# Copying the transposed causal attention weights of both octets on ScalarE, none on VectorE

## What is computed

```python
scores = jnp.einsum('bhid,bhjd->bhij', q, k)
rel = jnp.einsum('bhid,pd->bhip', q, rel_key)
rel_idx = jnp.clip(j - i + p - 1, 0, p - 1)
bias = jnp.take_along_axis(rel, ..., axis=3)
logits = jnp.where(causal[None, None], (scores + bias) * scale, -jnp.inf)
attn = jax.nn.softmax(logits, axis=-1)
out = jnp.einsum('bhij,bhjd->bhid', attn, v)
...
x = x + _layernorm(_L0_attn_ref(_layernorm(x), ...))   # causal attention
x = x + _layernorm(_L0_ffn_ref(_layernorm(x), ...))    # gated feed-forward, silu
x = x + _layernorm(_L1_attn_ref(_layernorm(x), ...))   # quaternion attention
x = x + _layernorm(_L1_ffn_ref(_layernorm(x), ...))    # 8 experts, 2 per token
```

## Time and profile before

| | us |
|---|---|
| median of 3 runs | 986.7 |
| lowest and highest | 984.15, 988.79 |
| the profiled execution | 992.06 |
| its span in the profile | 990.0 |

### The profile page before, as it was taken

The page is one execution under the profiler, slowest core; times in us unless marked ns, Lnnn a source line. Parts: engine busy times, 40 slices in busy tenths (PEclk is TensorE's granted clock), DMA queues, the critical chain, the costliest instruction groups (busy, mean ns, idle before and its releaser), DMA issues.

```text
span 990.0 us, 21425 instructions
## 1 busy us (share of the span) xinstructions
PE 776.4 (78%) x8384; PEld 558.3 (56%) x8384; DVE 499.9 (50%) x1656; ACT 456.7 (46%) x885; POOL 177.1 (18%) x306
## 2 busy tenths in 40 slices
PE   1678887787887889998998976788787767488994
PEld 0466766565765566665665654366443545267773
DVE  3266556556645465545446562647454536423315
ACT  1234352235454547665556653556844445332321
POOL 3200101000010000020000004233005553115411
PEclk9999999699997999998899997999977989979998
DMA  4400200000400001300000212011131110011101
GB/s 109 156 2 2 121 2 2 2 1 2 151 2 5 8 13 32 99 23 2 12 12 1 87 43 74 20 31 32 42 121 49 46 49 27 6 30 38 38 20 35
DMA packets 36440, 38.29 MB, mean 39 GB/s; under 512 B 8982, under 2 KB 26220, under 8 KB 36212
## 3 DMA queue, kind: packets, MB, share of 16 engines
q1 hardware_dynamic: 34548, 33.65, 11.3%
q0 software_dynamic: 1536, 3.15, 1.1%
q10 hardware_dynamic: 256, 0.13, 0.0%
HBM read 19.87 MB, written 16.91 MB: 37 GB/s over the span
## 4 chain that ended last, share of the span: by engine, by line
PE 51%; DVE 21%; issue 13%; ACT 8%; another core or an unknown queue 2%; ACTq 1%; DMA 1%; POOL 1%; SPq 0%; POOLq 0%; DVEq 0%
PE ps L1542 5%; PE ps L1687 5%; PE ps L1557 4%; PE ps L1545 4%; PE ps L1702 4%; PE ps L1470 3%; PE ps L1570 3%; PE ps L1762 3%; PE ps L1774 3%; ACT late L905 3%; DVE probsT L981 3%; PE ps L1637 2%; PE ps L1539 2%; DVE neg_max L1168 2%
## 5 line engine op out<-in xcount | busy, mean ns | idle before, releaser
L905 ACT ACTIVATE late<-ps,j_bias 128x512 f32<-128x512 f32 x256 | 173.3, 690 | 173.9 <-PE ps L1687 167.1
L1168 DVE TENSOR_REDUCE neg_max<-ps 128x2 f32<-128x32 f32 (+31 forms) x128 | 90.5, 707 | 147.8 <-PE ps L1548 143.4
L1687 PE MATMUL ps<-q_heads,k_parts 128*128 128x512 f32 x256 | 135.1, 546 | 22.1 <-ACT late L905 19.2
L832 ACT ACTIVATE probs<-ps,neg_max 128x16 f32<-128x16 f32 (+31 forms) x256 | 109.1, 483 | 23.7 <-DVE neg_max L1168 23.4
L756 ACT ACTIVATE probsT<-ps 128x128 f32<-128x128 f32 (+3 forms) x128 | 55.9, 437 | 126.8 <-PE ps L1557 113.1
L981 DVE COPY probsT<-ps 128x128 f32<-128x128 f32 (+3 forms) x173 | 75.1, 434 | 60.6 <-PE ps L1557 25.6
L1542 PE MATMUL ps<-kT_two,q_wide 64*64 64x262 f32 (+16 forms) x1024 | 74.3, 355 | 36.7 <-DVE probsT L981 26.2
L629 POOL TENSOR_TENSOR q_wide<-qT,eighth_mask 128x1024 f32<-128x1024 f32 x16 | 31.2, 1951 | 395.1 <-PE ps L1548 220.3
L1557 PE MATMUL ps<-ident,probs 128*128 128x128 f32 x640 | 96.9, 283 | 1.0 <-ACT probs L832 1.0
L1687 PEld LDWEIGHTS ps<-q_heads,k_parts 128*128 128x128 f32 x256 | 50.5, 205 | 71.9 <-ACT late L905 50.6
L1557 PEld LDWEIGHTS ps<-ident,probs 128*128 128x128 f32 x640 | 76.1, 144 | 16.6 <-issue 9.4
(11 more groups left out here) (265 smaller groups left out, 1315.7 us busy)
## 6 DMA issues: line engine op xcount, KB each, us to landing
k_parts<-k_half SPq DMA_DIRECT2D x16, 256.0 KB, 3.1
q_parts<-q_half SPq DMA_DIRECT2D x16, 256.0 KB, 3.5
k_parts<-k_parts SPq DMA_DIRECT2D x16, 256.0 KB, 3.1
q_heads<-q_parts SPq DMA_DIRECT2D x64, 64.0 KB, 2.1
x_by_expert<-q_heads SPq DMA_DIRECT2D x3, 960.0 KB, 7.6
probsT<-x_by_expert SPq DMA_DIRECT2D x45, 64.0 KB, 1.8
y_by_expert<-probsT SPq DMA_DIRECT2D x45, 64.0 KB
late<-in_L_ffn_w_dram SPq DMA_DIRECT2D x1, 2048.0 KB
```

What stands on the lines that cost most here:

```text
L832: nc.scalar.activation(probs[:, k, 0:L], ps[:, k, 0:L], ACT.Exp, bias=neg_max[:, n % 4, o:o + 1]).then_inc(exp_ready.sem, 1)
L905: nc.scalar.activation(head_probs[:, i % SLOTS, :], ps[:, banks[i % len(banks)], :], ACT.Exp, bias=j_bias[:]).then_inc(e2_ready.sem, 1)
L1168: nc.vector.tensor_reduce(neg_max[:, n % 4, :], ps[:, k:k + OCT, 0:QS * (n + 1)], axis=AXX, op=ALU.max, negate=True).then_inc(max_ready.se ...
L1687: mm(ps[:, banks[i % R], :], k_parts[:, hg, kc * P:(kc + 1) * P], q_heads[:, hg % 2, g, :], start=True, stop=True).then_inc(s2_ready.sem, 1)
```

## The change

ScalarE's generator issues two copies for each step, octet 0's and then octet 1's, ahead of the exponentials of the next step. VectorE's generator issues none; its piece in the odd slot keeps only the work that some steps have there (`copy_outT`, `divide_tile`). The two semaphores are renamed from the engine to the octet, and both are now raised by ScalarE; the waits for them stand where they stood.

```diff
--- before.py
+++ after.py
@@ -374,8 +374,8 @@
         max_ready = Signal(sem("max_ready"), NST)
         exp_ready = Signal(sem("exp_ready"), OCT * NST)
         pT_ps = Signal(sem("pT_ps"), OCT * NST)
-        pT_dve = Signal(sem("pT_dve"), NST)
-        pT_act = Signal(sem("pT_act"), NST)
+        pT_first = Signal(sem("pT_first"), NST)
+        pT_second = Signal(sem("pT_second"), NST)
         av_ps = Signal(sem("av_ps"), T)
         outT_ready = Signal(sem("outT_ready"), T)
         turned_ps = Signal(sem("turned_ps"), T)
@@ -836,7 +836,8 @@
                 yield
                 for n in range(NST):
                     yield
-                    copy_pT(act, copy, 1, pT_act, b, n)
+                    copy_pT(act, copy, 0, pT_first, b, n)
+                    copy_pT(act, copy, 1, pT_second, b, n)
                     if n + 1 < NST:
                         exps(n + 1)
                     if n >= SPT and n % SPT == 2:
@@ -1174,7 +1175,6 @@
                     if n + 1 < NST:
                         maxima(n + 1)
                     yield
-                    copy_pT(dve, copy, 0, pT_dve, b, n)
                     if n >= SPT and n % SPT == 0:
                         copy_outT(b, n // SPT - 1)
                     if n >= SPT and n % SPT == 1:
@@ -1526,8 +1526,8 @@
                     pe.wait_ge(qwide_ready.sem, qwide_ready.at(b, t + 1))
                     pe.wait_ge(b7_free, fill_no["R", b, 4 * t + 2] + 1)
                 if b * NST + n >= 2:
-                    pe.wait_ge(pT_dve.sem, pT_dve.at(b, n - 1))
-                    pe.wait_ge(pT_act.sem, pT_act.at(b, n - 1))
+                    pe.wait_ge(pT_first.sem, pT_first.at(b, n - 1))
+                    pe.wait_ge(pT_second.sem, pT_second.at(b, n - 1))
                 L = QS * (n + 1)
                 kT, kT_far = kT_two[:, b % 2, :], kT_far_two[:, b % 2, :]
                 blocks = [2 * (n % SPT) + z for z in range(2)]
@@ -1559,8 +1559,8 @@
                     last.then_inc(pT_ps.sem, 1)
 
             def weigh_values(b, t):
-                pe.wait_ge(pT_dve.sem, pT_dve.at(b, (t + 1) * SPT))
-                pe.wait_ge(pT_act.sem, pT_act.at(b, (t + 1) * SPT))
+                pe.wait_ge(pT_first.sem, pT_first.at(b, (t + 1) * SPT))
+                pe.wait_ge(pT_second.sem, pT_second.at(b, (t + 1) * SPT))
                 if b * T + t:
                     pe.wait_ge(attnT_ready.sem, attnT_ready.at(b, t))
                 for k in range(HG):
@@ -1674,8 +1674,8 @@
                 if b >= 1:
                     pe.wait_ge(e2_ready.sem, e2_ready.at(b, 0))
                 if R > 1:
-                    pe.wait_ge(pT_dve.sem, pT_dve.at(B, 0))
-                    pe.wait_ge(pT_act.sem, pT_act.at(B, 0))
+                    pe.wait_ge(pT_first.sem, pT_first.at(B, 0))
+                    pe.wait_ge(pT_second.sem, pT_second.at(B, 0))
                 for i in range(NCH + 5):
                     hg, kc, g = i // (KC * GH), i // GH % KC, i % GH
                     if i < NCH:
```

## The result

The changed kernel takes 950.4 us (median of four executions, 948.6 to 956.0), the kernel before 985.4 (982.8 to 988.8): a ratio of 0.965, 95% interval 0.960 to 0.971. Two repeats gave 951.5 against 984.0 (0.965, 0.962 to 0.969) and 964.3 against 993.8 (0.970, 0.966 to 0.974). Times are medians of all executions; ratios are of the means, without the few executions that fell in a slower state of the chip. So the sign and the main mechanism were right, and the size was too small by 10 to 15 us.

What follows compares the result with a forecast made beforehand. No engine is full: TensorE's work and the waits between its pieces bound the kernel. Terms 11 + 5 + 5 + 3 + 0 - 4 = 20 us take the median 986.7 to 966.7 us; range 953 to 982.

Steps and rivals of the forecast that it cites:

- What bounds it, what moves: Causal rounds: 128 copies leave VectorE (56 us less) for ScalarE (56 more); scores' waits on ScalarE grow to 30 to 40.
- (a): Four turns of tokens behind a normalisation: scores are done earlier, so TensorE turns right after it; 11 us gained.
- (b): Feed-forward's second normalisation, three times: scores stop waiting and L1094, which frees bank 7, starts earlier; 5 us gained.
- (c): Head's normalisation, three times: scores no longer wait for VectorE's copy behind L1045 and a maxima; 5 us gained.
- (d): Gate pieces, six times, where L1200 stands before VectorE's copy: both copies done 0.5 us earlier; 3 us gained.
- (e): The other 28 or so waits of TensorE for VectorE: up to 8 us more gain, counted at nothing.
- (f): Cost where ScalarE has no idle time, and through its later exponentials in rounds 2 and 3: 4 us, ends 2 and 22.
- The spacing: On ScalarE, the instruction following a 512-column copy starts 0.50 us after the copy's start, not 0.60.
- Behind 594 us the work is the same and simply starts earlier: After the four causal rounds: unchanged work, with no gain of its own in the sum.
- The clock: Rival in the causal rounds: joined gaps keep the granted clock low longer, costing 10 us of the gain, 977; chance 0.04.
- The range: Whole kernel: 953 us, from a gain of 34 with small costs, to 982, where the wait is handed on.

Runs made afterwards that it cites:

- second and third pairs: Kernel before and changed kernel, each run and traced again without any edit: 951.5 against 984.0 us, then 964.3 against 993.8 us.

## Why the prediction was too small

- *What bounds it, what moves.* Right. No causal copy of `probsT` by VectorE is left (its first one, at 596.4 us, is the later stage's); the waits for ScalarE's copies are 30.0 us, at the lower edge of the 30 to 40 expected; rounds 1 and 3 are shorter by 9 to 12, rounds 0 and 2 by 1 to 5. "ScalarE 56 us more" was wrong: 39, since copies in a row overlap. "VectorE 56 us less" was 50, of copies that had taken 62.3.
- *(a)* 11 forecast, 8.0 to 10.4 measured, some 5 of it at equal clock in the second and third pairs. The turns, rounds 1 and 3 of the first trace of the changed kernel:

```profile
174.09 1.12 DVE L1046 TENSOR_SCALAR xn<-x_all,moments,rstd 128x128 f32<-128x128 f32 x4
174.59 1.16 PE L1423 MATMUL ps<-ident,xn 128*128 128x128 f32 x4 [4.61 <-DVE xn L1046]
...
554.84 1.11 DVE L1046 TENSOR_SCALAR xn<-x_all,moments,rstd 128x128 f32<-128x128 f32 x4
555.34 1.00 PE L1423 MATMUL ps<-ident,xn 128*128 128x128 f32 x4 [0.70 <-DVE xn L1046]
```

  The turn now ends 0.54 and 0.39 us after the normalisation (2.57 and 3.5 before), as argued. In round 1 the wait ahead of it is as long as ever, 4.61 us for 4.59: it changed its name, and the gain is the scores that no longer stand behind it. The shortfall is round 2, steps 7 to 10, which gained between -1.0 and 0.7 us for 2.5, with 7 to 10 us of low clock around this very turn in both kernels, and the last turn, which gained 2.5 us in two pairs (3.9 in the first) for 3.8.
- *(b)* The term that was mis-sized, as shown above: 5 forecast, 11.5 measured. 4.8 us are three stretches of low clock that went away with the gaps; the other 6.7 are two waits of the scores in each round, where the forecast had priced one.
- *(c), (d)* Right, within 1 us each.
- *(e), (f)* Together -4 forecast, -1.7 twice and 1.7 once. This is a small net of larger parts: the steps that became longer add up to 11 to 12 us in each pair, some of it from low-clock stretches that moved. A single case of 0.15 us per step in 18 steps was too little for (f), and nothing too little for (e): steps 24 of round 1 and 25 of round 3, in none of (a) to (d), gained 1.9 and 1.2 us. The two errors mostly cancelled. The spacing on which (f) rested holds. Two copies of 512 columns, which would be 1.20 us one after the other:

```profile
259.96 1.08 ACT L756 ACTIVATE probsT<-ps 128x512 f32<-128x512 f32 x2 [0.67 <-PE ps L1557]
```

  That is 0.48 us to the start of the second and 0.60 for the second, as long as one alone. The Trainium skill (VectorE: DVE Perf Modes, the section on the TRN2 errata) has a fixed part in every copy out of PSUM, which made an estimate of 0.57 us for the first; the trace shows it is not paid in full between two copies in a row.
- *"Behind 594 us the work is the same and simply starts earlier."* The rounds explain 24.7 of 32.5 us on one chip and 24.5 of 29.5 on the other, and 27.1 of 35.0 in the first result. The 5 to 8 us that remain are what the sum lacks besides the clock in the rounds, and their cause stays open. Part of them goes with the clock: within the executions of before on the three chips (23, 13 and 29) the time rises by 0.17, 0.34 and 0.25 us for each us of low clock, and the changed kernel has 34 and 20 us less of it on the first and the last chip (98 for 132, 125 for 145). 10 us of that vanish in the rounds, where they are already counted, so it would explain 24 x 0.17 = 4 and 10 x 0.25 = 2.5 us, if the slopes hold between kernels. The traces don't show it: outside the rounds the three pairs differ by 9.0, 0.2 and -0.5 us, and from the copy of the section below to the end it took 386.3, 376.8 and 378.7 us before and 378.9, 377.8 and 386.0 after, the same in the mean, with no less low clock.
- *The clock.* I had put it at a small chance of costing 10 us. In the rounds there was 10 us less of it, worth some 5 us. The sign of that rival was wrong. That less idleness may end the low stretches sooner stands beside it in the prediction, but the sum had no term for it.
- *The range.* Its lower end, 986.7 - 34, isn't the sum of its own parts: (a) to (d) with (e) in full and (f) at 2 give 24 + 8 - 2 = 30 us, 957. The miss of 3 us would have been 6.

## What to carry to other kernels

A copy that frees PSUM for the next matmuls costs what stands before it in its engine's queue, not its own 0.4 us: look for every place where it follows a chain of small dependent instructions, count all of them, and give it to the engine that would otherwise wait for the same matmuls. Here that engine was good for one more copy, hardly for two. And where TensorE's gaps vanish while the granted clock is low in places, put the low clock into the range as a gain too: here 10 us of it went, worth some 5.

## What was not expected of the hardware

While POOL issues its eight indirect DMAs, some 1.27 us apart, the other engines can stand still although what they wait for is done. The third trace of before, then the second of the changed kernel:

```profile
596.56 1.17 POOL L676 DMA_INDIRECT x_by_expert<-xn,row_no  x1 [64.28 <-DVE row_no L1313]
...
600.75 0.27 PE L1570 MATMUL ps<-probsT,v_two 128*9 128x128 f32 x1 [0.31 <-issue]
...
605.63 0.96 POOL L676 DMA_INDIRECT x_by_expert<-xn,row_no  x1 [0.30 <-issue]
607.97 0.62 SPq L536 DMA_DIRECT2D kT_far_two<-in_L_ffn_b_dram  x2
607.98 0.69 DVE L981 COPY outT<-ps 128x512 f32<-128x512 f32 x1 [11.71 <-remote]
608.00 0.95 POOL L684 MEMSET b_two<- 128x1024 f32 x1 [1.42 <-remote]
608.01 1.26 ACT L905 ACTIVATE late<-ps,j_bias 128x512 f32<-128x512 f32 x2 [14.48 <-remote]
```

```profile
572.28 1.17 POOL L676 DMA_INDIRECT x_by_expert<-xn,row_no  x1 [59.80 <-DVE row_no L1313]
573.42 0.63 SPq L536 DMA_DIRECT2D kT_far_two<-in_L_ffn_b_dram  x2
573.43 0.69 DVE L982 COPY outT<-ps 128x512 f32<-128x512 f32 x1 [1.45 <-PE ps L1570]
```

In the first, L1570's last matmul ends at 601.0, and the copy that waits for it starts at 607.98, in the same 0.05 us as the next instruction of ScalarE, POOL and SP. In the second it starts at once. From the first indirect DMA to this copy it took 1.2 or 2.8 us in the four traces on the chip where before took 984 us, and 4.3 to 11.5 us in the eight on the other two chips, with different kernels in either group. In the mean that is 5.6 us more, about half of what those chips take longer. In the first trace of before it was 4.3 us. The change doesn't touch this place, but it took 4.3, 2.8 and 11.4 us before and 2.8, 1.2 and 4.3 in the changed kernel: 3.4 us in the mean that a pair of traces counts as gain. As the kernel with the change in rounds 2 and 3 alone had 11.5 us, and before on another chip 2.8, this may be chance. What holds the signals back was not tried.
